# A four-layer attention kernel on one core: mask products widened, rotations respaced, weight loads and closing sums moved into other stages

## The reference, cut to what matters

```
xn = layernorm(x)
x  = x + attention_l(xn) * silu(ffn_l(xn))          # l = 0 .. 3
```

## Time and profile before

| | us |
|---|---|
| median of 3 runs | 5402.67 |
| lowest, highest | 5399.36, 5404.75 |
| time of the profiled execution | 5403.82 |
| its span, first to last instruction | 5402.5 |
| PE busy in the span | 4711.6 (87%) |
| DVE, ACT, POOL busy | 3267.2, 2560.6, 2355.1 |
| mean granted TensorE clock | 0.934 |

### The profile page before, as it was taken

How to read it: one execution, slowest core, us unless ns; L and a number is a source line. 1 busy time by engine, 2 the same in 40 slices (tenths; PEclk the granted TensorE clock), 3 DMA queues, 4 the chain that set the end, 5 groups by cost and what they waited for, 6 DMA issues and landing times. The chain is left out here.

```text
span 5402.5 us, 69019 instructions
## 1 busy us (share of the span) xinstructions
PE 4711.6 (87%) x27372; PEld 2311.8 (43%) x27372; DVE 3267.2 (60%) x4327; ACT 2560.6 (47%) x3868; POOL 2355.1 (44%) x1372
## 2 busy tenths in 40 slices
PE   5899999968888688785979999994899999999996
PEld 3444444435565433332432222222445555555553
DVE  4756566526666676774157787865166655565563
ACT  2344444435555355553236666661244444444443
POOL 0455554546566067785000000000046666666664
PEclk8999999978998799997979999997899999999998
DMA  0000000010000000000000000000000000000000
GB/s 31 3 3 3 4 3 3 1 35 9 9 9 1 2 2 2 2 1 23 0 3 1 2 1 2 1 1 9 2 4 3 1 3 3 3 3 1 3 1 15
DMA packets 52003, 27.71 MB, mean 5 GB/s; under 512 B 30004, under 2 KB 47968, under 8 KB 51424
## 3 DMA queue, kind: packets, MB, share of 16 engines
q1 hardware_dynamic: 51680, 23.29, 1.6%
HBM read 22.23 MB, written 1.05 MB: 4 GB/s over the span
## 5 line engine op out<-in xcount | busy, mean ns | idle before, releaser
L780 DVE TENSOR_REDUCE L_part<-banks 128x2 f32<-128x1024 f32 (+2 forms) x1600 | 1882.0, 1189 | 995.0 <-PE banks L631 855.3
L765 ACT ACTIVATE L_weights<-banks 128x1024 f32<-128x1024 f32 (+1 forms) x1600 | 1581.5, 1001 | 1051.2 <-PE banks L663 838.6
L689 PE MATMUL banks<-L_weights,L_V 128*32 128x512 f32 (+3 forms) x6400 | 1500.1, 605 | 5.2 <-ACT L_weights L765 3.0
L987 POOL TENSOR_TENSOR L_wsum<-L_wsum,L_weights 128x1024 f32<-128x1024 f32 (+1 forms) x448 | 986.0, 2201 | 54.8 <-ACT L_weights L765 2.1
L970 POOL TENSOR_TENSOR L_wsum<-L_wsum,L_two 128x1024 f32<-128x1024 f32 x240 | 570.7, 2378 | 858.4 <-DVE L_two L954 855.7
L689 PEld LDWEIGHTS banks<-L_weights,L_V 128*64 128x64 f32 (+1 forms) x6400 | 283.6, 123 | 459.4 <-issue 397.8
L663 PE MATMUL banks<-L_QH,L_KH 64*128 64x512 f32 (+3 forms) x1664 | 432.2, 453 | 17.9 <-issue 10.2
L196 POOL MEMSET SACC<- 128x2048 f32 x4 | 7.2, 1804 | 987.1 <-POOLq L97 987.1
L631 PE MATMUL banks<-L_KH,L_QH 64*128 64x512 f32 (+3 forms) x1664 | 372.9, 429 | 31.0 <-ACT L_weights L765 17.5
L663 PE MATMUL banks<-L_QL,L_KH 64*128 64x512 f32 (+3 forms) x1664 | 372.5, 382 | 0.0
L663 PE MATMUL banks<-L_QH,L_KL 64*128 64x512 f32 (+3 forms) x1664 | 372.2, 381 | 0.0
(11 more groups left out here) (446 smaller groups left out, 6372.8 us busy)
## 6 DMA issues: line engine op xcount, KB each, us to landing
F_tab<-xpos SPq DMA_DIRECT2D x8, 512.0 KB, 3.8
F_h<-L_ffn_h_w SPq DMA_DIRECT2D x2, 1024.0 KB, 7.3
F_wqkv<-L_ffn_wqkv SPq DMA_DIRECT2D x2, 768.0 KB
L_cos<-rope_cos SPq DMA_DIRECT2D x1, 1024.0 KB, 5.1
L_sin<-rope_sin SPq DMA_DIRECT2D x1, 1024.0 KB, 7.1
out<-X SPq DMA_DIRECT2D x1, 1024.0 KB, 5.1
F_w<-L_ffn_w_w SPq DMA_DIRECT2D x3, 256.0 KB, 3.6
F_w<-L_ffn_w SPq DMA_DIRECT2D x2, 341.0 KB
```

Source lines behind the costliest of these rows:

```text
L689: mm = pe.e.matmul(O[r, c:BANK], self.V[g % 2][:, kt, h, :], self.W[x % self.NW][:, y, c:BANK], start=kt < starts, stop=kt >= tiles - starts)
L765: act.e.activation(self.W[x % self.NW][:, :, c:BANK], self.banks(it)[:, :, c:BANK], ACT.Exp, scale=self.scale).then_inc(self.exped, 1)
L780: dve.e.tensor_reduce(self.part[n % 3][:, pr, j, p, :], self.banks(it)[:, :, 0:wide], AX.X, ALU.max).then_inc(self.mx_read, 1)
L987: pool.e.tensor_tensor(acc[:, :, c:BANK], acc[:, :, c:BANK], W[:, :, c:BANK], ALU.add).then_inc(self.summed, 1)
```

## The change

It has these parts.

1. The Gate's mask is stored twice side by side; a score step issues two 512-column mask products first and adds the four score products on top.
2. `SPINS` has one rotation per step; `TURNS` of tiles 2 and 3 come one step later. The order within each step follows from the same sorting and cut.
3. `shift` copies first and takes bn_stats from the copy. The memset at L2027 is gone.
4. The Gate's loads are issued in `norm_layer(1)` (`ahead`), and so are those of the mixture of experts, with eight columns and two masks of attention 3, in `norm_layer(3)`.
5. `residual` of layers 0, 1 and 2 is now the beginning of the next `norm_layer` (`quarters`); the memset of `SACC` follows it, and is left out before layer 3.
6. `once_more` of the latent attention divides its 24 zeroing copies over ACT, DVE and POOL.
7. Layer 2: POOL adds `bo` to `xpt`, `GATE * ln_beta` to `X`, and multiplies `GATE` by gamma during the narrow attention. `attention2` keeps the sum with `SACC` and the norm.
8. Layer 3: the mlp's weights are loaded, `Wo` scaled, `bo` made and `SACC = XN + bo` written (POOL, PE, ACT) in the first stage of `attention3`; the sum after the attention is gone.

The diff, cut:

```diff
-def norm_layer(core, layer):
+def norm_layer(core, layer, ahead=None):
...
+        if ahead:
+            ahead(dve, pool, sp)
+        if layer:
+            quarters(core, dve, product, added)
+            dve.wait_ge(added, 4)
         norm.moments(dve, lambda i: core.X[:, i, :], 1e-5)
...
-        pool.e.memset(core.SACC[:, :, :], 0.0).then_inc(zeroed, 1)
+        if layer != 3:
+            pool.wait_ge(added, 4 if layer else 0)
+            pool.e.memset(core.SACC[:, :, :], 0.0)
...
+def quarters(core, dve, product, added):
     for i in range(4):
         s = slice(4 * i, 4 * i + 4)
         dve.e.tensor_tensor(core.GATE[:, s, :], core.GATE[:, s, :], core.SACC[:, s, :], ALU.mult).then_inc(product, 1)
         dve.wait_ge(product, i + 1)
         dve.e.tensor_tensor(core.X[:, s, :], core.X[:, s, :], core.GATE[:, s, :], ALU.add).then_inc(added, 1)
...
@@ LatentAttention.once_more
-        for t in self.KB + [self.QB]:
-            for r in self.AGAIN:
-                for b in range(4):
-                    dve.e.tensor_copy(t[r, b * BANK:(b + 1) * BANK], zero[r, :]).then_inc(zeroed, 1)
...
+        for n, r in enumerate(self.AGAIN):
+            if n:
+                pool.wait_ge(by_pool, 4)
+            for b in range(4):
+                s = slice(b * BANK, (b + 1) * BANK)
+                act.e.activation(self.QB[r, s], zero[r, :], ACT.Copy)
+                dve.e.tensor_copy(self.KB[0][r, s], zero[r, :]).then_inc(zeroed, 1)
+                pool.e.tensor_copy(self.KB[1][r, s], zero[r, :]).then_inc(by_pool, 1)
+        dve.wait_ge(zeroed, 9)
         for t in self.KB:
+            if t is self.KB[1]:
+                dve.wait_ge(by_pool, 8)
...
@@ NarrowAttention
+        for i, n in enumerate(("bo", "ln_gamma", "ln_beta")):
+            load(self.after_rows[:, i, :], self.io["L2_attn_" + n].partition_broadcast(P))
...
+    def gpsimd(self, pool):
...
+        chain(pool.e.tensor_scalar(self.after_rows[:, 1, :], self.after_rows[:, 1, :], self.positions.f[:, 4:5], None, ALU.mult))
+        chain.step(pool.e.tensor_tensor(xpt[:, :, :], xpt[:, :, :], over(0), ALU.add))
+        chain(pool.e.tensor_tensor(self.product_rows[:, :, :], core.GATE[:, :, :], over(2), ALU.mult))
+        chain.step(pool.e.tensor_tensor(core.X[:, :, :], core.X[:, :, :], self.product_rows[:, :, :], ALU.add))
+        chain(pool.e.tensor_tensor(core.GATE[:, :, :], core.GATE[:, :, :], over(1), ALU.mult))
...
@@ TransformerGate
-    SPINS = [(-5, 0, 1), (-5, 0, 0), (-4, 1, 1), (-3, 1, 0), (-3, 2, 1), (-2, 2, 0), (-1, 3, 1), (0, 3, 0)]
-    TURNS = [(-3, 0), (-1, 1), (0, 2), (2, 3)]
+    SPINS = [(-5, 0, 1), (-4, 0, 0), (-3, 1, 1), (-2, 1, 0), (-1, 2, 1), (0, 2, 0), (1, 3, 1), (2, 3, 0)]
+    TURNS = [(-3, 0), (-1, 1), (1, 2), (3, 3)]
...
-    def load(self):
+    def ahead(self, dve, pool, sp):
...
         for i in range(2):
-            load(self.mask[:, i, :], io["band_mask"].bitcast(BF16)[i])
+            for p in range(2):
+                load(self.mask[:, i, p, :], io["band_mask"].bitcast(BF16)[i])
...
-        mask = self.mask[:, min((4 * u + i) % 16, 1), :]
+        mask = self.mask[:, min((4 * u + i) % 16, 1), :, :].rearrange("p a k -> p (a k)")
+        for y in range(2):
+            pe.e.matmul(self.buffer(w)[:, y * BANK:(y + 1) * BANK], self.core.identb[:, :], mask, start=True, stop=False)
         for p in range(2):
             j = h // 2 + p
-            out = [self.buffer(w)[:, y * BANK + 256 * p:y * BANK + 256 * p + 256] for y in range(2)]
             for y in range(2):
-                r = slice(64 * y, 64 * y + 64)
-                pe.e.matmul(out[y], self.qT[(4 * u + i) % 3][r, j, :], self.kT[u % 2][r, j, i * P:(i + 2) * P], start=True, stop=False)
-            for y in range(2):
-                m = pe.e.matmul(out[y], self.core.identb[:, :], mask, start=False, stop=True)
+                r, out = slice(64 * y, 64 * y + 64), self.buffer(w)[:, y * BANK + 256 * p:y * BANK + 256 * p + 256]
+                m = pe.e.matmul(out, self.qT[(4 * u + i) % 3][r, j, :], self.kT[u % 2][r, j, i * P:(i + 2) * P], start=False, stop=p == 1)
         m.then_inc(self.s_made, 1)
...
-                self.chain.step(dve.e.bn_stats(self.st6[u % 2][:, i, :], self.ybanked(it)[:, 0:P]))
                 dve.e.tensor_copy(self.z[u % 2][:, i, :], self.ybanked(it)[:, 0:P]).then_inc(self.y_dve, 1)
+                self.yread(dve, it)
+                self.chain.step(dve.e.bn_stats(self.st6[u % 2][:, i, :], self.z[u % 2][:, i, :]))
...
-        pool.e.memset(self.core.SACC[:, :, :], 0.0)
...
@@ attention2
-        sp.wait_ge(loaded, 48)
-        dve.wait_ge(loaded, 48)
...
-        chain(dve.e.tensor_scalar(rows[:, 1, :], rows[:, 1, :], f[:, 4:5], None, ALU.mult))
         chain(dve.e.scalar_tensor_tensor(xpt[:, :, :], A[:, :, :], f[:, 2:3], xpt[:, :, :], ALU.mult, ALU.add))
-        chain(dve.e.tensor_tensor(xpt[:, :, :], xpt[:, :, :], over(0), ALU.add))
...
-        chain(dve.e.tensor_tensor(A[:, :, :], A[:, :, :], over(1), ALU.mult))
-        chain(dve.e.tensor_tensor(A[:, :, :], A[:, :, :], over(2), ALU.add))
...
@@ attention3, first stage
+            mlp.load(sp)
...
+            mlp.begin(pe, act, pool)
...
+    def begin(self, pe, act, pool):
...
+        pool.wait_ge(self.loaded, self.total)
+        pool.e.memset(self.ones[:, :], 1.0).then_inc(scaled, 1)
+        pool.e.tensor_tensor(self.Wo[:, :, :], self.Wo[:, :, :], self.bv[:, :].rearrange("p (g a) -> p g a", a=1).to_broadcast([P, 8, D]), ALU.mult).then_inc(scaled, 1)
+        pe.wait_ge(scaled, 2)
+        for g in range(8):
+            mm = pe.e.matmul(core.bank(2)[:, 0:P], self.ones[:, :], self.Wo[:, g, :], start=g == 0, stop=g == 7)
+        mm.then_inc(bv_made, 1)
+        act.wait_ge(bv_made, 1)
+        act.e.activation(self.bo[:, :], core.bank(2)[:, 0:P], ACT.Copy).then_inc(bo_copied, 1)
+        pool.wait_ge(bo_copied, 1)
+        pool.e.tensor_tensor(self.bo[:, :], self.bo[:, :], self.rows[:, 0, :], ALU.add).then_inc(bo_made, 1)
+        pool.wait_ge(bo_made, 1)
+        over = self.bo[:, :].rearrange("p (a d) -> p a d", a=1).to_broadcast([P, NT, D])
+        pool.e.tensor_tensor(core.SACC[:, :, :], core.XN[:, :, :], over, ALU.add).then_inc(summed, 1)
...
@@ program
-        residual(core)
-        norm_layer(core, 1)
         with ExitStack() as own:
-            TransformerGate(core, own, io).run()
+            gate = TransformerGate(core, own, io)
+            norm_layer(core, 1, gate.ahead)
+            gate.run()
...
+                moe = SoftMoe(core, own, io, gains, last)
+                norm_layer(core, 3, moe.ahead)
+                moe.run()
```

More of the change, by code:

```diff
@@ L207, in residual @@
         dve.e.tensor_tensor(core.X[:, s, :], core.X[:, s, :], core.GATE[:, s, :], ALU.add).then_inc(added, 1)
+def residual(core):
+    product, added = core.sems("product", "added")
+    pe, dve, act, pool, sp = core.engines()
+    quarters(core, dve, product, added)
     core.end()
@@ L1509, in run @@
         core = self.core
-        self.load()
         self.plan()
@@ L1551, in load @@
         sp.wait_ge(loaded, load.n)
-        core.end()
     def plan(self):
@@ L2287, in attention3 @@
             norm, turn = Norm(core, inner, "A3n"), Turn(core, "A3n")
-            loaded, made, src_made = core.sems("gains_loaded", "z_made", "src_made")
+            made, src_made = core.sems("z_made", "src_made")
             pe, dve, act, pool, sp = core.engines()
-            load = Loads(sp.e, loaded)
-            with nc.allow_non_contiguous_dma("columns of 128"):
-                for i, n in enumerate(("lnk_s", "lnk_b", "lnq_s", "lnq_b", "lnv_s", "lnv_b", "lnm_s", "lnm_b")):
-                    load(gains[:, i:i + 1], io["L3_attn_" + n].rearrange("(p a) -> p a", a=1))
-            load(last[0][:, :, :], io["last_q"].bitcast(BF16))
-            load(last[1][:, :, :], io["last_k"].bitcast(BF16))
-            sp.wait_ge(loaded, load.n)
+            mlp.load(sp)
             norm.moments(dve, lambda i: core.XN[:, i, :], 1e-5)
@@ L2368, in scalar @@
+    def scalar(self, act):
+        self.norm.root(act)
+        self.turn.scalar(act, self.yT, scale=self.gains[:, 6:7], bias=self.gains[:, 7:8])
         for c in range(4):
             for j in range(2):
-                act.wait_ge(up_made, 2 * c + j + 1)
-                act.wait_ge(down_made, c - 1)
-                act.e.activation(u[:, c % 2, j, :], core.bank(bank(c, j)), ACT.Gelu_apprx_tanh, bias=b1[:, j:j + 1]).then_inc(gelu_made, 1)
-    def tensor(pe):
-        pe.wait_ge(ones_made, 1)
-        pe.wait_ge(Wo_scaled, 1)
-        for g in range(8):
-            mm = pe.e.matmul(core.bank(2)[:, 0:P], ones[:, :], Wo[:, g, :], start=g == 0, stop=g == 7)
-        mm.then_inc(bv_made, 1)
-        turn.tensor(pe, z, z_made)
-        pe.wait_ge(turn.copied, 4)
-        pe.wait_ge(bo_made, 1)
+                act.wait_ge(self.up_made, 2 * c + j + 1)
+                act.wait_ge(self.down_made, c - 1)
```

(14 more changed lines are left out.)

183 lines of the change are left out of this document (83 added, 100 removed).

## The result

The changed kernel takes 5321.46 us (median of 4 runs, 5314.86 to 5325.29) beside 5401.37 us for the kernel before (median of 4): a ratio of 0.985, with a 95% interval of 0.9833 to 0.9867. That is 80 us less, where 94 were forecast; 5321 lies in the stated range. The profiled execution of the changed kernel took 5323.64 us with a span of 5322.3, so the two profiled executions differ by 80.2 us, and the table splits that by stages, each from its own first instruction to the next one's. The limits are again the barriers.

What follows compares the result with a forecast made beforehand. PE was taken to bound the Gate and the narrow and normed attention, DVE's chain or SP's queue the short stages between. Terms summing to -93.9 from 5403.8, less 1.1, gave 5309 us; range 5283 to 5346, from term bounds 5290 to 5330.

Steps and rivals of the forecast that it cites:

- the loads: Before the Gate: its loads, issued beside residual and norm, no longer take a stage of their own; -17.3 us.
- the closing sums: Layer 2: the wait for rows, the first product and three sums' work mostly go; -12.2 us.
- the last stage: Last layer: loads, scaling, PE's 16 products and two sums ahead of bn_stats all go; -15.2 us.
- The sources' stage: Start of attention 3: products, small sum and POOL's `SACC = XN + bo` moved there lengthen it; +5 us.
- rival 4: Narrow attention and sources' stage: each long POOL sum holds DVE, 14.7 us more, total 5324 us; chance 0.06.
- Gate, prologue: Gate's start: only one rotation stands before POOL's first product of the division; -6.5 us (0 to -9).
- No wait of `turn` for POOL: Sign expected in the Gate's chain of waits: `turn` never waits for POOL's rotations; no size given.
- Gate, units: Gate's steady state: POOL waits go, clock rises, `z` copy comes later; 4.5 us a unit times 7, -31.5 us.
- rival 3: Gate: POOL one rotation late makes every `turn` wait up to 4.1 us; total 5471 us; chance 0.02.
- the new sorting moves the cut: Gate, step 3: `shift` falls behind division and maxima, so DVE's copy of `z` starts 3.2 us later.
- Mask: Gate scores: wide mask products save 0.1 us a score over 64 scores; -6.4 us (0 to -13).
- Experts: Mixture of experts: weights loaded ahead remove DVE's wait at the stage's start; -7.2 us (-6 to -7.5).

Runs made afterwards that it cites:

- e4: Changed kernel with the mask again as four products of 256 columns behind the scores: 5325.39 us, ratio 0.987.
- e3: Changed kernel with only step 3's `shift` back ahead of table and division, rotations keeping their new places: 5323.64 us, ratio 0.9863.
- e9: Changed kernel with shift and table first in step 3 of a Gate unit, DVE's norm and root behind division and maxima: 5298.31 us, ratio 0.9814.
- e1: The changed kernel run again without any edit: 5323.86 us, ratio 0.9863.
- e5: Changed kernel with the Gate's rotations and transposes at their old steps: 5347.02 us, ratio 0.9902.
- e12: e9 plus all Gate rotations behind their step's division, DVE writing `SACC = XN + bo`, POOL's narrow-attention sums held back: 5286.40 us, ratio 0.9792.

## Why the prediction was right, and where not

**Boundaries.** The terms of the loads, the merged residuals, the closing sums and the last stage came within 1 us each; each was worked out from rows of the stage itself. The sources' stage cost 6.1 us where 5 were forecast. POOL's sum took 5.35 us, the 4.4 and the 1 us of hindrance that were booked; what the forecast lacked is POOL's scaling of `Wo`, which held one of DVE's operations, so that PE's transposes ended 1.6 us later in the stage and the sum began 1.0 us later than worked out. The narrow attention cost 3.2 for 2.3, by the mechanism of rival 4: two of the four sums held DVE in the prologue; at the other two DVE was waiting for PE.

**Gate, prologue.** -6.5 forecast. From the stage's start to the third transpose of the input it took 70.9 us and now takes 61.0: -9.9, just past the bound of -9. PE's wait for POOL's product fell from 7.0 to 0.2 us there, and from 15.0 to 1.9 us up to the fourth transpose. "No wait of `turn` for POOL" did not come true: up to the fourth transpose PE waits 8.1 us for `F_qn`, where it waited 5.9.

**Gate, units.** "Net 6.3 + 1.5 - 3.2 = 4.6, taken as 4.5, times 7". A unit became 5.0 us shorter (76.1 to 71.1, means of four), of which the mask is 0.4 to 0.6 by its price in e4, so the number for one unit was right, but partly by luck. Over these four units PE's wait for POOL went as forecast (25.2 us, 6.3 a unit, to nothing) and the one for `z` grew from 11.8 to 30.0, 4.5 a unit where 3.2 were forecast; PE's idle time in all fell by 1.2 a unit, not 3.1. Its busy time fell by 3.8 a unit, at a granted clock of 0.95 for 0.92, which is more than the 1.5 of clock and the mask together. The factor was wrong too: the last stretch, from the last transpose of the input to the end, went from 205.9 to 201.8 us, 4.1 for what the forecast counted as more than two units and the memset. PE was idle for 38.6 us of it and is for 35.7. The wait for POOL's product fell there from 11.4 to 0.9 us; the view of waits in that stretch of the changed kernel shows what stands in its place, beside 7.4 us for the one late copy of `z` (2.9 before):

```profile
PE banks L1756 <- DVE F_wts L1995: 6.5, 4, 5.2
PE banks L1730 <- POOL F_qn L2086: 5.8, 3, 2.5
...
PE banks L1803 <- DVE F_z L2034: 4.9, 2, 3.7
```

PE waits at `turn` for the q rotation one step before it, the mechanism of rival 3, three times, 5.8 us in all; the kernel before has no such wait there. That PE comes to it sooner for want of the products of a next unit is likely, and no run isolates it.

The reason given for the 3.2 us was half right. The copy does come late and PE does wait for it; but "the new sorting moves the cut" was named as the cause, and e3, which undoes just that, gained nothing. The forecast charged one row of the timeline for what the whole chain of DVE in that step costs. e9, which moved the chain itself, shortened the Gate by 21 us.

**Mask.** 0.05 to 0.08 us a score for 0.1: 3 to 5 us for 6.4.

**Experts.** "Loaded ahead, 7.2 go" is right for the start: DVE's first square starts at 3646.03, with the stage, and the stage with the loads put back took 185.0 us against 177.7 in e1, whose other parts have the same lengths. The step that failed is that the rest of the stage would keep its time: the clock took 5.8 us off the first part and put 11.2 on the combining. A stretch at 1.2 GHz costs this stage as much as the edit brings. Why it fell into the combining in most profiles was not settled.

**Normed attention.** +2.2 with the same instructions; the eleven experiments' stages lay between 1431.3 and 1434.3 us, the kernel before at 1431.9. No cause is claimed.

**The range and the rivals.** "Its own range, from the bounds of its terms, is 5290 to 5330" is not what the bounds give: added up, they reach from 5268 to 5370. And 5321 is nearer to the 5324 of rival 4 than to 5309, which is chance: the two stages that rival 4 speaks of missed by 2.0 us together, and the rest of the 14 is the Gate's last stretch and the clock in the experts.

## What to carry over

A stall that one row names may be only the place at which an engine's chain comes due: before an edit is charged or credited with it, ask what the other engine would still have to do if that row were moved. A steady gain per unit need not hold for the last units, where other waits come to the front. And a long elementwise operation moved to an idle POOL is not free where DVE has operations of the kinds that were held here: with two SBUF inputs, or tensor_scalar on SBUF. Where DVE had neither, it was free.

## What the runs showed of the hardware

**The clock differs between executions of the same instructions.** The experts' stage has the same instructions on PE, ACT and DVE in all profiles. The combining took 45.0 to 45.3 us in three of them (before, e5, e12) and 56.2 to 57.9 in ten. Windows of e5, and of e12, where the slow stretch stood in the part ahead of it:

```profile
3677.50:3799.10 121.60, 96.77 (x360) 51.71 (x360) 42.24 (x81) 21.17 (x33) 0.00 (x0) 0.85 0.00 1
3799.10:3844.20 45.10, 41.99 (x192) 23.85 (x192) 8.30 (x32) 14.03 (x19) 0.00 (x0) 0.99 0.00 1
```

```profile
3613.50:3739.20 125.70, 101.02 (x360) 54.23 (x361) 42.27 (x81) 21.18 (x34) 0.00 (x0) 0.80 0.00 0
3739.20:3784.50 45.30, 42.00 (x192) 23.83 (x192) 8.31 (x32) 14.01 (x19) 0.00 (x0) 0.99 0.00 1
```

The stage took 166.7 us in e5, 171.0 in e12, 176.5 to 177.8 in the others with early loads: 11 us between runs of one code, more than most of the edits here brought. In the changed kernel PE had been idle for 4.5 us in four gaps between 3753 and 3766.3 (it waits for DVE and ACT between small products, and at the barrier) before the clock fell to 1.2 GHz at 3768.5, and had worked without a gap before it rose at 3792.4. The kernel before has the same gaps at the end of the dispatch; there the clock fell at 3836.8, right behind the first of them, and was back after 6.8 us. What decides between the two is not shown.

**POOL and DVE in the Gate.** With rotations in every step, DVE's own half of the division became slower: 102 of its products between 1240 and 1710 us before, and 1220 and 1660 after, by form (total, mean ns):

```profile
L1962 DVE TENSOR_SCALAR F_wts<-F_wts,F_rden 128x256 f32<-128x256 f32 x102 | 84.6, 869 | 1.8
```

```profile
L1995 DVE TENSOR_SCALAR F_wts<-F_wts,F_rden 128x256 f32<-128x256 f32 x102 | 104.6, 1064 | 1.8
```

That is 0.39 us a step on the engine that the Gate now waits for, 20 us of DVE's time in this stretch. In e5, with the rotations at their old steps, the mean is 888 ns (1240 to 1710 us), so it is the respacing that makes them slow. The Trainium skill ("SBUF — State Buffer", section "Who interferes with whom") counts tensor_scalar among the operations that can contend with POOL for the shared ports; the rows agree.
